# A reordered prologue for a chain of modulated convolutions, with products of zeros on TensorE in front of the first R and the first T

## The chip, the cores and the metric

The kernel runs on one core of one Trainium2 chip. The metric is the time of one launch in microseconds, as the median of several runs. The profile is one more execution, taken with the hardware profiler on. PE is TensorE's matmul row, PEld its weight loads, DVE is VectorE, ACT is ScalarE, POOL is GpSimd and SP the engine that issues most of the transfers.

## The reference, cut to what matters

Thirty-two samples of 64 channels and 1024 positions pass through four modulated 1-D convolutions with three taps (same, up by two with a blur, same, down by two with a blur). The result is added to the input. All of it is float32.

```python
def _layer(x, style, w, b, mw, mb, typ):
    s = style @ mw.T + mb
    weight = SCALE * w * s[:, None, :, None]
    demod = lax.rsqrt(jnp.sum(weight * weight, axis=(2, 3)) + EPS)
    weight = weight * demod[:, :, None, None]
    # 'same': conv, + b;  'upsample': transposed conv stride 2, + b, blur (1,3,3,1);
    # 'downsample': blur (1,3,3,1), conv stride 2, + b
out = x
for i, typ in enumerate(('same', 'upsample', 'same', 'downsample')):
    out = _layer(out, style, weights[i], biases[i], mod_w[i], mod_b[i], typ)
return x + out
```

## The kernel before, in words

The four layers are linear in the sample, so the kernel composes their taps into one filter per sample and applies that once. It works on eight groups of four samples (`QUADS`, index `q`). For a group, `compose_R` multiplies layer 2's taps (`V_st`) with layer 3's scaled taps (`A_sb`), `compose_H` brings in the blurred layer 1 (`F_st`) and `compose_T` layer 0 (`W0_st`). ACT empties PSUM after each, with the sample's scales (`evac_R`, `evac_H`, `evac_T`). The result is the filter `Tw`. DVE (first group) or POOL (later groups) adds the identity of the residual and sums of blocks to it (`add_ident`, `sum_blocks`). Then five products with the input follow, by a fast algorithm on differences of the input: `product_a2`, `product_bc2`, `product_a13`, `product_bc1`, `product_bc3`. Their moving operands are `x3` (ACT, `make_x3`), `dx_sb` (POOL, `make_dx`), `d_sb` and `dd_sb` (DVE, `make_d`, `make_dd`). DVE merges the products into the output tile (`make_s`, `make_e`, `finish`). In the loop over groups the work of group q+1 and q+2 on R, H and T stands between the products of group q.

Ahead of the loop stands a prologue, and the change is there. TensorE multiplies zeros four times (`pe_warm`, line 436), turns the modulation weights, forms the styles (452), turns the sums of squared weights (458), turns layer 3's taps (`put["GT"]`, 463), forms the demodulation sums (471) and blurs layer 1's taps in two parities (`blurred_taps`, 419, `put["FT"]`). Then come R of group 0, the turned taps of layers 0 and 2 (`transposed`, 410), R of group 1, a small product for the constant part (640), H of group 0, layer 3's blurred taps (`blurred_halves`, 429, for `o_st`), a second small product (649), the first of the edge products (`edge_x0`, 599), T of group 0, H of group 1, and the last small product (659, `put["oc"]`). The edges of the samples are computed apart in four small products, with POOL adding the offsets.

DVE makes the scales: styles, then `dt_`, then a square root on ACT (709), then `demodulation`, which refines it in four small instructions and yields `e2` (needed by `make_A`, hence by R), `a0` (by `evac_H`) and `id` (by `add_ident`). `s0` is a copy of the first layer's style that `evac_T` takes as its scale, `e1` the scale of `evac_R`. POOL copies `V_st` and `W0_st` out of the loaded weights, makes `dx_sb` for group 0, and builds `y_st`, the blurred taps for the edges, with `coef` and `prod`. The order of the work on each engine is written out by hand, and semaphores join the engines.

Of the kernel before, what the change touches and what calls it, by code (L numbers as in the profile page):

```python
# [10 lines left out]
P = 128  # L11
# [15 lines left out]
def modulated_conv_kernel(nc, x, cond, weights, biases, mod_w, mod_b, out):  # L27
# [18 lines left out]
    with ctx:  # L46
# [9 lines left out]
        def bufs(make, name, n, *a):  # L56
# [27 lines left out]
        coef = sb("coef", [C, len(BLUR), 1])  # L84
        prod = sb("prod", [C, K, len(BLUR), C])
# [61 lines left out]
                                            "GT", "FT", "oT", "x0e", "ye", "ze", "oe", "yc", "zc", "oc")}  # L147
        coef_made = sem("coef_made")
        blur_step = sem("blur_step")
        copied = {n: sem(f"copied_{n}") for n in ("styleT", "wsumT", "w0T", "G_mv", "V_st", "W0_st", "F_st", "w2T", "o_st")}  # L150
        made = {n: sem(f"made_{n}") for n in ("cid", "bias", "wsum", "style2", "s0", "dt", "e2", "e1", "a0", "vec", "y_st",
# [88 lines left out]
        def _(pool):  # L240
# [6 lines left out]
            for j, v in enumerate(BLUR):  # L247
                pool.memset(coef[:, j], v / 4).then_inc(coef_made, 1)
# [4 lines left out]
            pool.wait_ge(w_loaded, 16)  # L253
            for l, to, name in ((2, V_st, "V_st"), (0, W0_st, "W0_st")):
                of = wn[:, l].rearrange("o i k -> o k i")
                for h in range(2):
                    pool.tensor_copy(to[h * C:(h + 1) * C], of).then_inc(copied[name], 1)
                    pool.wait_ge(copied[name], h + 1)

            make_dx(pool, 0)  # L260

            pool.wait_ge(zeroed, 7)
            pool.wait_ge(coef_made, len(BLUR))
            n = len(BLUR)
            for k in range(K):
                pool.tensor_tensor(prod[:, k], wn[:, 1, :, k].unsqueeze(1).to_broadcast([C, n, C]),
                                   coef[:].to_broadcast([C, n, C]), ALU.mult).then_inc(blur_step, 1)
            for k in range(K):
                pool.wait_ge(blur_step, K + k)
                pool.tensor_tensor(y_st[0:C, k:k + n], y_st[0:C, k:k + n], prod[:, k], ALU.add).then_inc(blur_step, 1)  # L270
            pool.wait_ge(blur_step, 2 * K)
            pool.tensor_copy(y_st[C:P, 4:6], y_st[0:C, 2:4]).then_inc(made["y_st"], 1)

# [5 lines left out]
            pool.wait_ge(made["s0"], 1)  # L279
# [127 lines left out]
        def _(pe):  # L407
# [6 lines left out]
            def blurred_taps(l, bank, cid, n, par):  # L414

                for k in range(K):
                    for h in range(2):
                        b0 = 2 + par - k
                        ins = pe.matmul(bank[h * C:(h + 1) * C, 0:n * C], wn[:, l, :, k],
                                        cid[:, b0:b0 + 2 * n - 1:2, :], start=(k == 0), stop=(k == K - 1),  # L420
                                        skip_group_check=True)
                return ins
# [10 lines left out]

            pe.wait_ge(warm_made, 1)
            for _ in range(4):
                pe.matmul(p_h[:, 1, 0:256], pe_warm[:, 0:P], pe_warm[:], start=True, stop=True)
# [12 lines left out]
            ins.then_inc(put["bias"], 1)  # L449
            pe.wait_ge(copied["styleT"], 1)  # L450
# [4 lines left out]
            for half in (1, 0):  # L455
# [3 lines left out]
                ins.then_inc(put["wsumT"], 1)  # L459

# [5 lines left out]

            for half in (1, 0):
                pe.wait_ge(copied["wsumT"], 2 - half)
                pe.wait_ge(made["style2"], 1)
                for l in (2 * half, 2 * half + 1):  # L470
                    ins = pe.matmul(p_c[1 - half][0:C, 0, 256 + l * B:256 + (l + 1) * B], wsumT[:, l], style2[:, l, :],
                                    start=True, stop=True)
                ins.then_inc(put["demod"], 1)

            pe.wait_ge(made["cid"], 1)
            pe.wait_ge(made["s0"], 1)
            pe.wait_ge(made["bias"], 1)
# [126 lines left out]
            def edge_y():  # L604
                pe.wait_ge(made["x0e"], 1)
                pe.wait_ge(made["y_st"], 1)
# [29 lines left out]
            pe.wait_ge(copied["F_st"], 2)  # L636
            compose_R(1, p_h)
# [7 lines left out]
            blurred_halves(3, p_y[:, 1], cid1, 3).then_inc(put["oT"], 1)  # L645
            pe.wait_ge(made["z_st"], 6)
            pe.wait_ge(made["yc"], 1)
            for k in range(3):
                ins = pe.matmul(p_x[:, 1, 0:B], z_st[:, k, :], yc[:], start=(k == 0), stop=(k == 2))
            ins.then_inc(put["zc"], 1)  # L650
            pe.wait_ge(copied["w2T"], 1)
            edge_x0()
            compose_T(0)
            compose_H(1)
# [31 lines left out]
        def _(act):  # L686
# [8 lines left out]

            act.wait_ge(put["styleT"], 1)
# [8 lines left out]
            copy(G_mv[:], p_y[:, 1, 0:K * C].rearrange("p (a c) -> p a c", c=C), copied["G_mv"])  # L705
            for n, half in enumerate((1, 0)):
# [48 lines left out]
            act.wait_ge(put["FT"], 1)  # L755
            copy(F_st[:, 0:NF:2], p_x[:, 1, 0:5 * C].rearrange("p (a c) -> p a c", c=C), copied["F_st"], 1.0 / 32)
# [3 lines left out]
            act.wait_ge(put["FT"], 2)  # L760
            copy(F_st[:, 1:NF:2], p_h[:, 0, 0:4 * C].rearrange("p (a c) -> p a c", c=C), copied["F_st"], 1.0 / 32)
            make_A(1)
            act.wait_ge(made["e1"], 2)
            evac_R(0, p_k)
            act.wait_ge(put["w2T"], 1)
            copy(w0T[:], p_y[0:C, 0, 0:3 * C].rearrange("p (k c) -> p k c", c=C), copied["w0T"])
            copy(w2T[:], p_y[0:C, 0, 256:256 + 3 * C].rearrange("p (k c) -> p k c", c=C), copied["w2T"])
            evac_R(1, p_h)
            make_A(2)
# [22 lines left out]
        def _(dve):  # L792
# [48 lines left out]
            dve.wait_ge(put["bias"], 1)  # L841
            ts(biases2[:].rearrange("p j l -> p (j l)"), p_h[:, 1, 0:2 * LAYERS], 1.0, name="bias")
# [28 lines left out]
            for h, rows in enumerate(halves):  # L871
                ts(pgi(W_S0, h), gi(style[rows, 0], h), 1.0, name="s0")
            for n, half in enumerate((1, 0)):
                of = slice(2 * half, 2 * half + 2)
                dve.wait_ge(put["demod"], n + 1)
                for rows in halves:
                    ts(dt_[rows, of], p_c[1 - half][0:C, 0, 256 + 2 * half * B:256 + 2 * (half + 1) * B]
                       .rearrange("p (l b) -> p l b", b=B), SCALE2, EPS, ALU.mult, ALU.add, "dt")
            for h, rows in enumerate(halves):
                tt(pgi(W_E1, h), gi(style[rows, 2], h), gi(style[rows, 1], h), ALU.mult, "e1")  # L880

# [82 lines left out]
            for h, rows in enumerate(halves):  # L964
                tt(pgj(W_E2, h), gj(style[rows, 3], h), gj(dm[rows, 2], h), ALU.mult, "e2")
            dve.wait_ge(sqrt_done, 2)
# [3 lines left out]
            ts(vec[:, V_B0, 0:B], dm[:, 1, :], bias[:, 0:1], name="vec")  # L970
            demodulation(3, 4)
# [17 lines left out]
            make_d(0)  # L989
# [5 lines left out]
            dve.wait_ge(zeroed, 7)  # L995
            scale_edge("x0e", one_below_the_other(p_y), x0e[0:C], V_A0, WX0)
# [3 lines left out]
            sum_blocks(dve, 0)  # L1000
            dve.wait_ge(made["d3"], 2)
# [6 lines left out]
            make_dd(0)  # L1008

            for q in range(QUADS):  # L1010
                make_s(q)
                if q + 1 < QUADS:
                    make_d(q + 1)
# [6 lines left out]
                finish(q, 1, bank_bc3(q), bc3_done, y13_made)  # L1020
                if q + 1 < QUADS:
# [26 lines left out]
```

## Time and profile before

| | us |
|---|---|
| median of 3 runs | 163.07 (162.77 to 163.49) |
| the profiled execution, its own time | 164.6 |
| its span, first to last instruction | 162.5 |
| PE busy in the span | 149.3 |
| DVE busy | 117.5 |
| POOL busy | 68.7 |
| ACT busy | 57.1 |

The profiled execution took 1.1 us longer than the slowest of the three runs, and 2.1 us of its time lie outside the span. In the views, start and duration are microseconds from the span's start; a row of the timeline merges instructions of one kind in a row, with "x" for how many, and a matmul in float32 shows as two records. The granted clock is a share of TensorE's full 2.4 GHz, so 0.50 is 1.2 GHz.

### The profile page before, as it was taken

To read this page: it belongs to the slowest core of one execution; us is meant where nothing else is said; L and a number is where in the kernel's file an instruction comes from. 1 tells how busy PE (TensorE), PEld (TensorE's weight loads), DVE (VectorE), ACT (ScalarE), POOL (GpSimd) and SP (SyncE) were. 2 spreads that over 40 slices of the span, in tenths; PEclk is the share of its full clock that TensorE was granted. 3 is DMA by queue.
4 is the path that set the end of the run, shared out by engine and by line. 5 is a ranking of instruction groups with operands and counts; after the bars stand their busy time and mean duration, and the time that the engine had idled before them with its cause. 6 is when DMAs were issued, how large, how long until landed. Compare 5 with 4: busy or idle time off the path is not lost.

```text
span 162.5 us, 5859 instructions
## 1 busy us (share of the span) xinstructions
PE 149.3 (92%) x2585; PEld 117.5 (72%) x2585; DVE 117.5 (72%) x185; ACT 57.1 (35%) x118; POOL 68.7 (42%) x101
## 2 busy tenths in 40 slices
PE   7995999879999999999999999999999999989920
PEld 5562998555578656685889699879988997957810
DVE  7999745298786367697775877489747885789760
ACT  3222543545405512444346416541454234402000
POOL 8696060730385056692680086009402920540000
PEclk9965579999999999999999999999999999999995
DMA  4968100006001600059706920890190038005526
GB/s 122 346 152 225 53 0 4 0 4 237 25 0 21 249 0 4 0 183 325 268 11 135 292 97 0 200 316 11 31 226 9 4 68 193 6 0 114 148 48 210
DMA packets 9400, 17.62 MB, mean 108 GB/s; under 512 B 4736, under 2 KB 5280, under 8 KB 9376
## 3 DMA queue, kind: packets, MB, share of 16 engines
q1 hardware_dynamic: 9312, 17.24, 36.9%
q8 instruction: 20, 0.33, 0.8%
q14 instruction: 4, 0.03, 0.1%
q10 hardware_dynamic: 64, 0.02, 0.0%
HBM read 8.87 MB, written 8.39 MB: 106 GB/s over the span
## 4 chain that ended last, share of the span: by engine, by line
PE 78%; DVE 14%; issue 3%; ACT 1%; DVEq 0%; ACTq 0%
PE p_c L540 44%; PE p_k L507 11%; PE p_h L525 11%; PE p_k L490 5%; DVE e_sb L925 2%; DVE ot L937 2%; DVE pvec L815 1%; PE p_h L490 1%; DVE cid L815 1%; PE p_h L617 1%; PE p_h L610 1%; DVE pvec L811 1%; DVE Tw L214 1%; PE p_k L530 1%; DVE cid L828 1%
## 5 line engine op out<-in xcount | busy, mean ns | idle before, releaser
L540 PE MATMUL p_c<-dd_sb,Tw 64*64 64x256 f32 x504 | 30.3, 376 | 0.7 <-DVE e_sb L925 0.7
L925 DVE SCALAR_TENSOR_TENSOR e_sb<-p_c,pvec,s_sb 128x512 f32<-128x512 f32 x32 | 21.8, 744 | 7.3 <-PE p_c L540 7.3
L540 PEld LDWEIGHTS p_c<-dd_sb,Tw 64*64 64x64 f32 x504 | 22.4, 132 | 5.6 <-DVE e_sb L925 1.1
L214 POOL TENSOR_TENSOR Tw<-Tw,di_sb 128x128 f32<-128x128 f32 x7 | 3.2, 460 | 52.4 <-ACT Tw L738 52.4
L937 DVE SCALAR_TENSOR_TENSOR ot<-p_c,pvec,e_sb 128x508 f32<-128x508 f32 x28 | 19.9, 754 | 7.2 <-PE p_c L540 7.2
L507 PE MATMUL p_k<-R_sb,F_st 64*64 64x192 f32 (+1 forms) x576 | 22.1, 302 | 0.7 <-ACT Tw L735 0.7
L507 PEld LDWEIGHTS p_k<-R_sb,F_st 64*64 64x64 f32 x576 | 20.3, 135 | 1.4 <-issue 0.9
L914 DVE SCALAR_TENSOR_TENSOR s_sb<-p_c,pvec,t_sb 128x512 f32<-128x512 f32 x16 | 11.3, 746 | 12.9 <-PE p_c L540 12.9
L540 PE MATMUL p_c<-d_sb,Tw 64*64 64x256 f32 x320 | 19.9, 386 | 0.0
L906 DVE TENSOR_TENSOR dd_sb<-d_sb 128x2064 f32<-128x2064 f32 x8 | 19.9, 2487 | 0.0
L540 PE MATMUL p_c<-dx_sb,Tw 64*64 64x256 f32 x320 | 19.0, 376 | 0.3 <-DVE ot L937 0.3
L525 PE MATMUL p_h<-H_sb,W_st 64*64 64x448 f32 (+1 forms) x192 | 19.2, 518 | 0.0
L899 DVE TENSOR_TENSOR d_sb<-xin 128x2072 f32<-128x2072 f32 x8 | 18.4, 2306 | 0.0
L234 POOL TENSOR_TENSOR dx_sb<-xin 128x1032 f32<-128x1032 f32 x8 | 17.2, 2146 | 1.1 <-DMA xin<-in_x_dram 1.0
L540 PEld LDWEIGHTS p_c<-dx_sb,Tw 64*64 64x64 f32 x320 | 14.0, 133 | 3.7 <-issue 1.2
L540 PEld LDWEIGHTS p_c<-d_sb,Tw 64*64 64x64 f32 x320 | 13.7, 132 | 3.0
L721 ACT ACTIVATE R_sb<-p_k,pvec 128x320 f32<-128x320 f32 x14 | 6.6, 524 | 25.8 <-PE p_k L490 25.8
L752 ACT ACTIVATE t_sb<-p_c,pvec 128x256 f32<-128x256 f32 x16 | 8.2, 560 | 18.5 <-PE p_c L540 18.5
L525 PEld LDWEIGHTS p_h<-H_sb,W_st 64*64 64x64 f32 x192 | 8.8, 133 | 6.7 <-issue 6.2
L728 ACT ACTIVATE H_sb<-p_k,pvec 128x448 f32<-128x448 f32 x16 | 9.3, 630 | 11.3 <-PE p_k L507 11.3
L540 PE MATMUL p_c<-x,Tw 64*64 64x256 f32 x192 | 12.0, 376 | 1.0 <-DVE Tw L226 1.0
L735 ACT ACTIVATE Tw<-p_k,pvec 128x64 f32<-128x64 f32 x16 | 4.2, 310 | 21.5 <-PE p_k L530 21.5
(146 smaller groups left out, 195.3 us busy)
## 6 DMA issues: line engine op xcount, KB each, us to landing
xin<-in_x_dram SPq DMA_DIRECT2D x16, 512.0 KB, 5.3
out_dram<-ot SPq DMA_DIRECT2D x14, 512.0 KB, 6.2
out_dram<-ot SPq DMA_DIRECT2D x4, 256.0 KB, 3.5
wn<-in_L_cond_weights_dram SPq DMA_DIRECT2D x1, 192.0 KB, 3.5
mwn<-in_L_cond_mod_w_dram SPq DMA_DIRECT2D x1, 128.0 KB, 2.3
xe<-in_x_dram SPq DMA_DIRECT2D x2, 64.0 KB, 9.4
cn<-in_cond_dram ACTq DMA_DIRECT2D x1, 16.0 KB, 2.2
bn<-in_L_cond_mod_b_dram ACTq DMA_DIRECT2D x1, 1.0 KB
```

The costliest lines, as they stand in the source:

```text
L234: eng.tensor_tensor(dx_sb[q % 2][:], view(a, 1, ((XW, 2), (4, 2), (4, NI))), view(a, 3, ((XW, 2), (0, 2), (4, NI))), ALU.subtract).then_in ...
L490: ins = pe.matmul(bank[i * C:(i + 1) * C, j, b * C:(b + K) * C], V_st[rows, K - 1 - b, :], A_sb[q % 2][rows, i], start=(b == 0), stop=(b = ...
L507: ins = pe.matmul(p_k[j * C:(j + 1) * C, i, to * C:(to + n) * C], F_st[rows, f, :], R_sb[q % 2][rows, j, par::2], start=(f == 0), stop=(f ...
L525: pe.matmul(p_h[i * C:(i + 1) * C, j, first * C:(first + n) * C], W0_st[rows, k, :], H_sb[rows, i, 0:n], start=(k == 2), stop=(k == 0), sk ...
L540: ins = pe.matmul(bank[j * C:(j + 1) * C, i], Tw[q % NW][rows, blk, j, :], moving(rows, j, n), start=(n == 0), stop=(n == len(blocks) - 1) ...
L728: act.activation(H_sb[:, i], p_k[:, i, 0:NH * C].rearrange("p (a c) -> p a c", c=C), ACT.Copy, scale=pcol(W_A0, 2 * q + i)).then_inc(H_eva ...
L752: act.activation(t_sb[q % 2][:, i], p_c[q % 2][:, i, 0:NQ], ACT.Identity, bias=pcol(W_C, 2 * q + i), scale=pcol(W_D3, 2 * q + i)).then_inc ...
L899: dve.tensor_tensor(d_sb[q % 2][:], view(a, 0, ((XW, 2), (2, 2), (2, ND))), view(a, 1, ((XW, 2), (0, 2), (2, ND))), ALU.subtract).then_inc ...
L906: dve.tensor_tensor(dd_sb[:].rearrange("p j t s n -> p (j t) s n"), view(a, 0, ((ND, 4), (2, 2), (2, NI))), view(a, 1, ((ND, 4), (0, 2), ( ...
L914: dve.scalar_tensor_tensor(out=s_sb[:, i], in0=p_c[(q + 1) % 2][:, i].rearrange("p (n h) -> p n h", h=2), scalar=pcol(W_D3, 2 * q + i), in ...
L925: dve.scalar_tensor_tensor(out=e_sb[:, i, w], in0=p_c[q % 2][:, i, w * NQ:(w + 1) * NQ].unsqueeze(2) .to_broadcast([P, NQ, 2]), scalar=pco ...
L937: dve.scalar_tensor_tensor(out=ot[q % NO_T][:, i, 4 + par:4 + par + 2 * n - 1:2], in0=bank[:, i, 2:2 + n], scalar=pcol(W_D3, 2 * q + i), i ...
```

## The change

The prologue is put in another order. POOL no longer copies `V_st` and `W0_st` (ACT does) nor builds `y_st` (four products on TensorE and two copies on ACT do), and its `make_dx(0)` waits for `a0`. On TensorE the blurred taps of the first parity are spread over three places, the demodulation sums come ahead of layer 3's turned taps, the turned taps of layers 0 and 2 come ahead of R, and `edge_x0` and the second small product come behind T of group 0. On ACT `evac_T(0)` follows `make_x3(0)`, and the two square roots follow the copies of `G_mv` and of half of `F_st`. On DVE `s0`, `e1`, `make_d(0)`, `make_dd(0)`, `make_d(1)` and the edge scaling of `x0e` come later. `keep_busy` multiplies zeros: three times ahead of R of group 0, once ahead of T of group 0.

```diff
 # POOL
-            pool.wait_ge(w_loaded, 16)
-            for l, to, name in ((2, V_st, "V_st"), (0, W0_st, "W0_st")):
-                    pool.tensor_copy(to[h * C:(h + 1) * C], of).then_inc(copied[name], 1)
+            pool.wait_ge(made["a0"], 2)
             make_dx(pool, 0)
-            for k in range(K):
-                pool.tensor_tensor(prod[:, k], wn[:, 1, :, k]..., coef[:]..., ALU.mult).then_inc(blur_step, 1)
-            for k in range(K):
-                pool.tensor_tensor(y_st[0:C, k:k + n], y_st[0:C, k:k + n], prod[:, k], ALU.add).then_inc(blur_step, 1)
-            pool.tensor_copy(y_st[C:P, 4:6], y_st[0:C, 2:4]).then_inc(made["y_st"], 1)
 # TensorE
+            def keep_busy(bank, times, n):
+                for _ in range(times):
+                    pe.matmul(bank[:, 0:n], pe_warm[:, 0:P], pe_warm[:, 0:n], start=True, stop=True)
+            blurred_taps(1, p_h[:, 0], cid2, 5, 0, 0)            # ahead of the styles
+            sums_turned(1)
+            sums_turned(0)
+            blurred_taps(1, p_h[:, 0], cid2, 5, 0, 1)
+            (demodulation sums, then GT)
-            pe.wait_ge(made["s0"], 1)
-            blurred_taps(1, p_x[:, 1], cid2, 5, 0).then_inc(put["FT"], 1)
-            blurred_taps(1, p_h[:, 0], cid2, 4, 1).then_inc(put["FT"], 1)
+            blurred_taps(1, p_h[:, 0], cid2, 5, 0, 2).then_inc(put["FT"], 1)
+            for k in range(K):
+                ins = blurred_taps(1, p_x[:, 0], cid2, 4, 1, k)
+            ins.then_inc(put["FT"], 1)
+            transposed(0, p_y[:, 0], 0)
+            transposed(2, p_y[:, 0], 256).then_inc(put["w2T"], 1)
+            pe.wait_ge(made["dt"], 4)
+            for j in range(len(BLUR)):
+                ins = pe.matmul(p_x[0:C, 1, j * C:(j + K) * C], cid1[:, 2 + j], wn[:, 1].rearrange("o i k -> o k i"),
+                                start=(j == 0), stop=(j == len(BLUR) - 1), skip_group_check=True)
+            ins.then_inc(put["yst"], 1)
...
+            pe.wait_ge(made["bias"], 1)
+            keep_busy(p_h[:, 1], 3, 256)
             compose_R(0, p_k)
-            transposed(0, p_y[:, 0], 0)
-            transposed(2, p_y[:, 0], 256).then_inc(put["w2T"], 1)
             pe.wait_ge(copied["F_st"], 2)
             compose_R(1, p_h)
...
             blurred_halves(3, p_y[:, 1], cid1, 3).then_inc(put["oT"], 1)
+            pe.wait_ge(R_evac, 4)
+            keep_busy(p_h[:, 1], 1, 256)
+            compose_T(0)
             (second small product, line 649 before)
+            compose_H(1)
             edge_x0()
-            compose_T(0)
-            compose_H(1)
 # ACT
+            act.wait_ge(w_loaded, 16)
+            copy_taps(2, V_st, "V_st")                           # ahead of the modulation weights
...
             copy(G_mv[:], ...)
+            act.wait_ge(put["FT"], 1)
+            copy(F_st[:, 0:NF:2], p_h[:, 0, 0:5 * C]..., copied["F_st"], 1.0 / 32)
             (the two square roots)
...
+            (F_st of the other parity, w2T, then make_A(0), make_A(1), the two copies into y_st)
             evac_R(0, p_k)
             evac_R(1, p_h)
-            make_A(2)
+            copy_taps(0, W0_st, "W0_st")
             evac_H(0)
+            make_x3(0)
+            act.wait_ge(made["s0"], 2)
             evac_T(0)
-            make_x3(0)
+            make_A(2)
             evac_H(1)
 # DVE
-            (s0 ahead of dt, e1 ahead of the demodulation; now behind a0 and behind e2)
-            make_d(0)
             (zc)
-            scale_edge("x0e", ...)
             add_ident(dve, 0)
             sum_blocks(dve, 0)
+            scale_edge("x0e", ...)
             (the two steps of W_C, named "c")
-            make_dd(0)
+            make_d(0)
             for q in range(QUADS):
                 make_s(q)
+                if q == 0:
+                    make_dd(0)
...
                 finish(q, 1, bank_bc3(q), bc3_done, y13_made)
+                if q == 0:
+                    make_d(1)
```

## Rows read from the trace of the kernel before

**Rows 1.** The chain of waits in order of time: start, duration, what ran.
```profile
15.43 0.81 ACT A_sb L715 x2
...
16.37 2.20 PE p_k L490 x24
...
35.26 3.69 PE p_c L540 x64
...
47.49 0.97 PE p_k L490 x24
...
51.49 2.50 PE p_k L507 x72
```

**Rows 2.** Timeline of TensorE's matmuls, 0 to 37 us.
```profile
1.20 3.78 PE L436 MATMUL p_h<-pe_warm 128*128 128x256 f32 x8 [1.20 <-DVE pe_warm L822]
...
7.47 0.75 PE L463 MATMUL p_c<-ident,wn 64*64 64x64 f32 x12
...
8.66 3.28 PE L419 MATMUL p_c<-cid,wn 64*64 64x320 f32 x12
11.66 2.84 PE L419 MATMUL p_h<-cid,wn 64*64 64x256 f32 x12
...
18.32 1.37 PE L410 MATMUL p_c<-ident,wn 64*64 64x64 f32 x11
...
24.79 1.23 PE L429 MATMUL p_c<-cid,wn 64*64 64x192 f32 x12
...
26.73 1.16 PE L599 MATMUL p_c<-xse,w0T 64*64 64x224 f32 x9
...
27.91 2.31 PE L525 MATMUL p_h<-H_sb,W_st 64*64 64x448 f32 x21
...
31.09 2.73 PE L507 MATMUL p_k<-R_sb,F_st 64*64 64x192 f32 x72 [0.74 <-ACT Tw L735]
33.75 0.54 PE L659 MATMUL p_c<-zc,o_st 128*64 128x32 f32 x12
...
36.60 2.34 PE L540 MATMUL p_c<-dx_sb,Tw 64*64 64x256 f32 x40
...
41.03 2.46 PE L540 MATMUL p_c<-d_sb,Tw 64*64 64x256 f32 x40
```

**Rows 3.** Stretches: engines' busy us, granted clock, DMA share, GB/s.
```profile
9.00:9.50 0.50, 0.50 (x4) 0.30 (x2) 0.50 (x1) 0.00 (x0) 0.50 (x1) 0.50 1.14 248
...
22.00:22.50 0.50, 0.50 (x11) 0.50 (x14) 0.16 (x1) 0.50 (x2) 0.50 (x2) 0.50 0.00 0
...
23.00:23.50 0.50, 0.50 (x21) 0.50 (x17) 0.50 (x5) 0.43 (x2) 0.16 (x1) 1.00 0.00 0
```

**Rows 4.** Timeline of DVE in the prologue.
```profile
8.39 2.12 DVE L815 TENSOR_SCALAR pvec<-style 64x16 f32<-64x16 f32 x2
...
23.57 2.30 DVE L899 TENSOR_TENSOR d_sb<-xin 128x2072 f32<-128x2072 f32 x1
...
28.20 0.81 DVE L811 TENSOR_TENSOR x0e<-p_c,vec 64x224 f32<-64x224 f32 x2 [0.88 <-PE p_c L599]
28.93 0.28 DVE L208 TENSOR_TENSOR di_sb<-ident,pvec 128x128 f32<-128x128 f32 x1
32.13 1.21 DVE L214 TENSOR_TENSOR Tw<-Tw,di_sb 128x128 f32<-128x128 f32 x1 [2.92 <-ACT Tw L738]
```

**Rows 5.** Timeline of POOL in the prologue.
```profile
8.40 2.08 POOL L234 TENSOR_TENSOR dx_sb<-xin 128x1032 f32<-128x1032 f32 x1 [0.98 <-DMA xin<-in_x_dram]
...
29.09 1.23 POOL L298 TENSOR_TENSOR x0e<-x0e,vec 64x224 f32<-64x224 f32 x2 [5.92 <-DVE x0e L811]
...
31.01 2.17 POOL L234 TENSOR_TENSOR dx_sb<-xin 128x1032 f32<-128x1032 f32 x1
```

**Rows 6.** Timeline of ACT in the prologue.
```profile
25.19 1.16 ACT L728 ACTIVATE H_sb<-p_k,pvec 128x448 f32<-128x448 f32 x2 [1.75 <-PE p_k L507]
...
30.42 0.52 ACT L735 ACTIVATE Tw<-p_k,pvec 128x64 f32<-128x64 f32 x2 [3.86 <-PE p_k L530]
```

More of the change, by code:

```diff
@@ L146, in modulated_conv_kernel @@
         put = {n: sem(f"put_{n}") for n in ("styleT", "bias", "w2T", "wsumT", "style", "demod",
[L147 to L151, printed above, removed]
+                                            "GT", "FT", "oT", "yst", "x0e", "ye", "ze", "oe", "yc", "zc", "oc")}
+        copied = {n: sem(f"copied_{n}") for n in ("styleT", "wsumT", "w0T", "G_mv", "V_st", "W0_st", "F_st", "w2T", "o_st", "y_st")}
+        made = {n: sem(f"made_{n}") for n in ("cid", "bias", "wsum", "style2", "s0", "dt", "e2", "e1", "a0", "vec",
                                               "z_st", "zc", "xse", "x0e", "ye", "ze", "yc", "c", "oe", "oep", "e_read",
@@ L277, in _ @@
                 pool.tensor_copy(dst, w2T[:, k]).then_inc(made["z_st"], 1)
-            pool.wait_ge(made["s0"], 1)
+            pool.wait_ge(made["z_st"], 6)
+            pool.wait_ge(made["style2"], 1)
             pool.wait_ge(e_loaded, 32)
@@ L412, in transposed, with blurred_taps @@
                 return ins
[L414 to L421, printed above, removed]
+            def blurred_taps(l, bank, cid, n, par, k):
+                for h in range(2):
+                    b0 = 2 + par - k
+                    ins = pe.matmul(bank[h * C:(h + 1) * C, 0:n * C], wn[:, l, :, k],
+                                    cid[:, b0:b0 + 2 * n - 1:2, :], start=(k == 0), stop=(k == K - 1),
+                                    skip_group_check=True)
                 return ins
@@ L432, in blurred_halves @@
                 return ins
+            def keep_busy(bank, times, n):
+                for _ in range(times):
+                    pe.matmul(bank[:, 0:n], pe_warm[:, 0:P], pe_warm[:, 0:n], start=True, stop=True)
             pe.wait_ge(warm_made, 1)
-            for _ in range(4):
-                pe.matmul(p_h[:, 1, 0:256], pe_warm[:, 0:P], pe_warm[:], start=True, stop=True)
+            keep_busy(p_h[:, 1], 4, 256)
             pe.wait_ge(ident_made, 1)
@@ L449, in _ @@
             ins.then_inc(put["bias"], 1)
+            pe.wait_ge(w_loaded, 16)
+            pe.wait_ge(made["cid"], 1)
+            blurred_taps(1, p_h[:, 0], cid2, 5, 0, 0)
             pe.wait_ge(copied["styleT"], 1)
@@ L453, in _, with sums_turned @@
             ins.then_inc(put["style"], 1)
-            for half in (1, 0):
+            def sums_turned(half):
                 pe.wait_ge(made["wsum"], 2 - half)
@@ L459, in _ @@
                 ins.then_inc(put["wsumT"], 1)
+            sums_turned(1)
+            sums_turned(0)
+            blurred_taps(1, p_h[:, 0], cid2, 5, 0, 1)
+            for half in (1, 0):
+                pe.wait_ge(copied["wsumT"], 2 - half)
+                pe.wait_ge(made["style2"], 1)
+                for l in (2 * half, 2 * half + 1):
+                    ins = pe.matmul(p_k[0:C, half, 256 + l * B:256 + (l + 1) * B], wsumT[:, l], style2[:, l, :],
+                                    start=True, stop=True)
+                ins.then_inc(put["demod"], 1)
             for a in range(K):
@@ L605, in edge_y @@
                 pe.wait_ge(made["x0e"], 1)
-                pe.wait_ge(made["y_st"], 1)
+                pe.wait_ge(copied["y_st"], 2)
                 pe.wait_ge(T_evac, 8)
@@ L694, in _, with copy_taps @@
             act.activation(sqrt_warm[:], xin[0][:, 0, 0:1], ACT.Sqrt)
+            def copy_taps(l, to, name):
+                for h in range(2):
+                    copy(to[h * C:(h + 1) * C], wn[:, l].rearrange("o i k -> o k i"), copied[name])
+            act.wait_ge(w_loaded, 16)
+            copy_taps(2, V_st, "V_st")
             act.wait_ge(put["styleT"], 1)
@@ L870, in _ @@
             dve.wait_ge(dve_step, n_style)
-            for h, rows in enumerate(halves):
-                ts(pgi(W_S0, h), gi(style[rows, 0], h), 1.0, name="s0")
             for n, half in enumerate((1, 0)):
@@ L876, in _ @@
                 for rows in halves:
-                    ts(dt_[rows, of], p_c[1 - half][0:C, 0, 256 + 2 * half * B:256 + 2 * (half + 1) * B]
+                    ts(dt_[rows, of], p_k[0:C, half, 256 + 2 * half * B:256 + 2 * (half + 1) * B]
                        .rearrange("p (l b) -> p l b", b=B), SCALE2, EPS, ALU.mult, ALU.add, "dt")
-            for h, rows in enumerate(halves):
-                tt(pgi(W_E1, h), gi(style[rows, 2], h), gi(style[rows, 1], h), ALU.mult, "e1")
             def demodulation(l0, l1):
@@ L965, in _ @@
                 tt(pgj(W_E2, h), gj(style[rows, 3], h), gj(dm[rows, 2], h), ALU.mult, "e2")
+            for h, rows in enumerate(halves):
+                tt(pgi(W_E1, h), gi(style[rows, 2], h), gi(style[rows, 1], h), ALU.mult, "e1")
             dve.wait_ge(sqrt_done, 2)
@@ L970, in _ @@
             ts(vec[:, V_B0, 0:B], dm[:, 1, :], bias[:, 0:1], name="vec")
+            for h, rows in enumerate(halves):
+                ts(pgi(W_S0, h), gi(style[rows, 0], h), 1.0, name="s0")
             demodulation(3, 4)
@@ L1000, in _ @@
             sum_blocks(dve, 0)
+            dve.wait_ge(zeroed, 7)
+            scale_edge("x0e", one_below_the_other(p_y), x0e[0:C], V_A0, WX0)
             dve.wait_ge(made["d3"], 2)
```

51 lines of the change are left out of this document (16 added, 35 removed).

## The prediction

> **What bounds the kernel now.** I read the chain of waits first. From 35 us to about 140 us it is TensorE with hardly a break, its products, R, H and T one behind the other in an order written by hand; two of its rows are R of a later group at 0.97 us and H at 2.50 us [rows 1]. Nothing in that stretch is changed except the place of DVE's differences for the first two groups. So the change is worth what it moves the start of the first group's second product, 36.60 in the timeline [rows 2], if no new wait follows. Ahead of it the chain goes through ACT's A (ends at 16.23), R at 16.37, and the first product at 35.26 [rows 1].
>
> Then the stretches with their clock: 0.50, the 1.2 GHz level, from 9.0 us to about 22.5, and 1.00 from 23.0 [rows 3]. Line 419 ran through the fall and stayed at the low level, twelve records in the 3.00 us from 8.66 to 11.66. The level rose after both first R and the start of H. In the first five microseconds the column says 1.00, but the eight records of zeros took 3.78 us, 0.47 us each for 256 columns, which is the low level's pace [rows 2].
>
> Last, DVE beside POOL. Two copies of 64x16 (`s0`) took 2.12 us, ending with POOL's `dx_sb` at 10.48; the first step on `Tw` took 1.21 us, where another of 128x128 took 0.28, ending just behind POOL's next `dx_sb` at 33.18 [rows 4, 5]. So instructions of the two on SBUF exclude each other here.
>
> **The change part by part, up to R.** On DVE the stall of 1.9 us behind `dx_sb` leaves (`s0` moves behind `a0`), and `y_st` no longer competes with the demodulation. A, made at 16.23 before, could be there at 14.3 or earlier. But TensorE now has more to do ahead of R. Its first eight records of blurred taps fit where it waits for the styles and their squares, so I leave the end of the demodulation sums at 8.66. From there, in order:
>
> - Layer 3's turned taps, 0.75 us [rows 2]: to 9.4.
> - Four records of the third tap, 0.25 each: 1.0.
> - Twelve of the other parity: 3.00 x 256/320 = 2.4, or 2.84 by their own row with its drain; 2.5.
> - Twelve turned taps of layers 0 and 2: eleven took 1.37; 1.3.
> - `y_st`, eight records of 192 columns on one tile alone, not in the trace. By the zeros 0.47 x 192/256 = 0.35 each, by the turned taps three times 0.11 or 0.12; 2.6 with the drain left out. Bounds: 1.3 at the high level, 2.8.
> - Zeros, six records: 3.78 x 6/8 = 2.8 with the drain, 2.6 without; 1.3 at the high level.
>
> At the low level that is 10.0 us, so R starts at 19.4, not 16.37. ACT makes A behind the copy of w2T, whose product ends at 9.4 + 4.8 = 14.2, so A is done near 15.6. By this TensorE does not wait in front of R at all; it would get there at 16.8 without the zeros, and they stand on the path for 2.6 us. The copies that ACT takes over from POOL lie in its waits ahead of the styles and ahead of H; uncovered they'd cost a few tenths each.
>
> What the zeros buy is the clock. Before, R took 1.95 us at the low level (16.37 to 18.32), later 0.97 [rows 1, 2]. If the level rises as R starts, both R and the small product behind them (0.35, an estimate: six records of two thirds of the last small product's twelve) end at 19.4 + 0.97 + 0.97 + 0.35 = 21.7, ACT emptying the first R beside the second, and H, 2.50, at 24.2. Before, H ended at 24.79, where line 429 starts. That is 0.6 gained. If both R still run low, H ends 1.96 later, at 26.15: 1.4 lost. The first zeros, four products, ran low to their end; the level after them was high by line 419's start at the latest. I take the rise inside the first R, at a third: 0.3 later, H's end at 24.5.
>
> The Trainium skill, page "TensorE: Matmul & The Clock Gate", Part 1, says that the default state is throttled and activity releases the throttle. The trace agrees for the first zeros but not for line 419, busy without a gap for 5.8 us and low throughout [rows 2, 3]. By that rule alone the new prologue, in which TensorE hardly pauses, would run high and end near 156.8; by the row it runs low to R, 162.0.
>
> **From H's end, called h.** ACT's copies of H end at 25.19 + 1.16, which is h + 1.56 [rows 6]. TensorE fills this with line 429 (1.0 without its drain) and the one product of zeros (two records of 0.47 at the low pace of line 436, half at the high one, 0.5): hidden, and 0.4 late if the level is low; and `edge_x0` no longer stands in front of T. T starts at h + 1.6. From T's start to ACT's first copy it is 2.5 (27.91 to 30.42), from there to DVE's first step 1.7: h + 5.8. DVE's sums took 3.13 us to 35.26; with POOL idle the first takes 0.28 instead of 1.21, so they end at h + 8.0. TensorE meanwhile runs H of group 1 (0.67 behind the first copy, 2.66 long) to h + 7.45, `edge_x0` 1.18 to h + 8.6, the last small product 0.45 to h + 9.05 [rows 2]. The first product starts there, against h + 10.47 before, and ends 1.34 later, h + 10.4.
>
> The second product then waits for `c`, and that chain is late now: DVE's x0e starts 1.47 behind `edge_x0`'s start, at h + 8.9, and ends at h + 9.7 [rows 2, 4]. Two steps from PSUM of 64x16 take 0.4, two more on SBUF as much (estimate: the pair of `s0` without its stall, 0.2 each), but POOL starts its two sums of x0e, 0.6 each [rows 5], so each comes behind one of these: `c` at h + 11.05. Without that contention it would be h + 10.5, and the wait 0.1. I take 11.1, against 36.60 - 24.79 = 11.8 before. Gain 0.7.
>
> The rest is covered: `make_d(0)`, 2.30, ends near h + 14, and the third product needs it 4.43 behind the second's start (36.60 to 41.03), at h + 15.5. `make_dd(0)` has the third product and the edge product in front of its reader. In group 0's end DVE makes two differences in a row while TensorE runs the next group's first product, H and second. POOL now waits for `a0`, which comes with A, near 15; queued behind that wait are `dx_sb` (2.08), the copies into `z_st` and the edge scaling `xse`, whose readers stand behind T, 10 us later. SP and its transfers are not moved, and its next loads that look at these differences belong to groups 4 and later.
>
> Sum: 0.6 - 0.3 + 0.7 = 1.0 us. The profiled execution's 164.6 would be 163.6; the median lies 1.5 under the profiled one, so from 163.07 I come to **162.0**. Half a per cent, about 0.8 us, is what a measurement can tell here.
>
> **The rivals.**
>
> - *The clock rises too late.* R and R of group 1 run low as they did before [rows 3], and the zeros only delay them: 1.4 lost, 0.7 won, 163.8. It decides from where both R have more than about 0.7 us of low level behind the forecast. For it: the rise came only behind both R before. Against it: then 1.2 us of turned taps on single tiles stood between them, now the zeros lead straight in. Chance 0.25, spread from 162.4 to 163.9.
> - *The clock does not fall at 9.* The products of blurred taps in the waits keep the level, all 10.0 us take 5.0, R starts at 14.4, and A (14.3 or earlier) is just there. Gain 0.6 + 0.7 + 5.0 = 6.3: 156.8. For it: TensorE is much busier between 5.5 and 9 than before. Against it: line 419 alone didn't raise the level. Chance 0.2; a fall one stretch later would land between.
> - *POOL's second difference goes in front of `make_d(0)`.* Both ask for SBUF near h + 11.6. If POOL's 2.17 goes first, d ends at h + 16.1, the third product is 0.6 late: 162.6. Chance 0.1.
> - *The zeros do nothing*, because R waits for A longer than I think: A past 19.4 would be 3.8 late. R is then where it is anyway and the other gains stay; its chance is inside the forecast's.
>
> The forecast itself has 0.45, from 161.5 (no contention for `c`, rise at R's start) to 162.4. Faster by over 0.5%: most of the forecast 0.38, the clock that stays 0.2, a little of the others: 0.6. Within: 0.06 + 0.13 + 0.08, 0.27. Slower: half of the late rise, 0.13. The range, 157.0 to 163.6, leaves out the lower half of the clock that stays (0.1) and the last of the late rise (0.08).
>
> **What would show it.** The clock should read 0.50 from about 9 to 19 and 1.00 by 20.5; the first R near 19.4, lasting under 1.5 us; line 436's new records 0.43 us apart; no wait of R for A. T should start 1.6 behind H, DVE's first step on `Tw` take 0.3, and the second product wait for `c` about 0.7. R near 14.4 with a high clock, or a low clock past 21, would make the forecast wrong.

## The result, and the profile after

The changed kernel takes 165.06 us (median of 4, 164.70 to 166.93), the kernel before 163.26 beside it (162.77 to 163.49): 1.0094, with a 95% interval of 1.0049 to 1.0140. It is slower by 0.9%, where 162.0 was forecast. Twelve more executions of the same kernel gave 165.12 against 163.37, 1.0056 (1.0024 to 1.0089). Executions over 1.5% above the fastest of their kernel count in the medians here, but not in the ratios.

The profiled execution of after took 166.93 us, the longest of its six, with a span of 164.9. So I show the profile of the repeated run too (165.56, span 163.8), which is nearer the median.

Timeline of TensorE's matmuls in the profile after (start, duration, line, what, how many records; in brackets a wait), beside [rows 2]:

```profile
6.07 1.33 PE L396 MATMUL p_h<-cid,wn 64*64 64x320 f32 x4
7.33 1.06 PE L436 MATMUL p_c<-cT,mwT 128*64 128x32 f32 x8
...
8.88 1.33 PE L396 MATMUL p_h<-cid,wn 64*64 64x320 f32 x4
10.01 0.89 PE L453 MATMUL p_k<-style,wsumT 64*64 64x32 f32 x7
...
12.41 2.92 PE L396 MATMUL p_c<-cid,wn 64*64 64x256 f32 x12
15.12 1.48 PE L388 MATMUL p_c<-ident,wn 64*64 64x64 f32 x12
16.41 2.76 PE L470 MATMUL p_c<-wn,cid 64*64 64x192 f32 x8
19.10 2.93 PE L414 MATMUL p_h<-pe_warm 128*128 128x256 f32 x6
21.95 1.94 PE L483 MATMUL p_k<-A_sb,V_st 64*64 64x192 f32 x24
23.72 1.15 PE L483 MATMUL p_h<-A_sb,V_st 64*64 64x192 f32 x24
...
27.58 1.24 PE L406 MATMUL p_c<-cid,wn 64*64 64x192 f32 x12
28.75 0.70 PE L414 MATMUL p_h<-pe_warm 128*128 128x256 f32 x2
29.39 2.38 PE L518 MATMUL p_h<-H_sb,W_st 64*64 64x448 f32 x24
...
36.92 1.53 PE L533 MATMUL p_c<-x,Tw 64*64 64x256 f32 x24
38.88 2.40 PE L533 MATMUL p_c<-dx_sb,Tw 64*64 64x256 f32 x40 [0.43 <-issue]
```

No row from 6.07 to 36.92 has a bracket: no wait of TensorE shows there. The zeros (L414, 19.10) and then R (L483, 21.95) begin as soon as the row ahead ends. R began at 16.37 before, so it is 5.6 later; the second product, 36.60 before, is 2.3 later, nearly as much as the span grew (164.9 against 162.5). From the second product to the end of the span it is 125.9 us before and 126.0 after: the loss is made ahead of it.

The chain of waits in the same profile, where [rows 1] had ACT's A just ahead of R:

```profile
6.14 1.26 PE p_h L396 x4
...
8.96 1.26 PE p_h L396 x4
...
12.77 2.56 PE p_c L396 x12
15.33 1.28 PE p_c L388 x12
16.61 2.56 PE p_c L470 x8
19.17 2.86 PE p_h L414 x6
22.02 1.86 PE p_k L483 x24
```

From 6.14 to R it is TensorE alone. ACT and POOL are out of it, as their own timelines show, beside [rows 5, 6]: A for the first two groups, on ACT, is done at 18.35, 3.6 ahead of R, and POOL's difference starts as soon as `a0` is there.

```profile
16.87 1.48 ACT L720 ACTIVATE A_sb<-G_mv,pvec 128x192 f32<-128x192 f32 x4
```
```profile
17.17 2.06 POOL L230 TENSOR_TENSOR dx_sb<-xin 128x1032 f32<-128x1032 f32 x1 [12.94 <-DVE pvec L820]
```

DVE, beside [rows 4]: it waits for the styles on TensorE (1.04 ahead of 8.43), `s0` stalls behind POOL once more (2.25, harmless here), and the first step on `Tw` takes 0.29 instead of 1.21.

```profile
8.43 0.28 DVE L820 TENSOR_TENSOR style<-p_c,biases 64x128 f32<-64x128 f32 x1 [1.04 <-PE p_c L436]
...
17.22 2.25 DVE L824 TENSOR_SCALAR pvec<-style 64x16 f32<-64x16 f32 x2
...
33.71 0.29 DVE L210 TENSOR_TENSOR Tw<-Tw,di_sb 128x128 f32<-128x128 f32 x1 [0.32 <-ACT Tw L743]
```

For the clock I read the repeated run, by stretches as in [rows 3] (the last three columns are granted clock, DMA share and GB/s). In after's own profile the column says 1.00 up to the rise, though the zeros took 0.48 us a record there, the low level's pace; its first entry stands at 23.49.

```profile
9.00:9.50 0.50, 0.50 (x4) 0.23 (x1) 0.00 (x0) 0.00 (x0) 0.00 (x0) 0.50 0.99 317
21.00:21.50 0.50, 0.50 (x2) 0.00 (x0) 0.47 (x2) 0.00 (x0) 0.50 (x2) 0.50 0.00 0
21.50:22.00 0.50, 0.50 (x11) 0.43 (x14) 0.47 (x3) 0.00 (x0) 0.29 (x1) 0.76 0.00 0
```

And the repeated run's TensorE:

```profile
5.85 0.79 PE L396 MATMUL p_h<-cid,wn 64*64 64x320 f32 x4
7.32 0.65 PE L436 MATMUL p_c<-cT,mwT 128*64 128x32 f32 x8 [0.68 <-ACT mwT L684]
...
8.46 1.33 PE L396 MATMUL p_h<-cid,wn 64*64 64x320 f32 x4
9.58 0.90 PE L453 MATMUL p_k<-style,wsumT 64*64 64x32 f32 x7
...
18.68 2.93 PE L414 MATMUL p_h<-pe_warm 128*128 128x256 f32 x6
21.54 1.28 PE L483 MATMUL p_k<-A_sb,V_st 64*64 64x192 f32 x24
...
37.80 2.39 PE L533 MATMUL p_c<-dx_sb,Tw 64*64 64x256 f32 x40 [0.42 <-issue]
```

Here the clock was high from 4.67 to 8.09 and from 21.74 (the trace's own entries for the clock, finer than the stretches). Four records of blurred taps (L396) take 0.79 in the high stretch and 1.33 behind it. So one kernel gives two prologues, by where the level changes.

The wait of 0.68 ahead of the styles (L436) has a cause that before had not. ACT now copies `V_st` before it copies the turned modulation weights (`mwT`, 6.89 to 7.27), and that copy waits for the weights to land:

```profile
5.81 0.97 ACT L684 ACTIVATE V_st<-wn 64x192 f32<-64x192 f32 x2 [2.16 <-DMA wn<-in_L_cond_weights_dram]
```

In the nine other profiles in which ACT makes this copy it starts between 4.59 and 4.91, so the late landing belongs to this execution. In before's profile `mwT` was copied at 5.88 without a look at these weights, and the styles stood at 6.32:

```profile
6.32 0.65 PE L452 MATMUL p_c<-cT,mwT 128*64 128x32 f32 x8 [0.35 <-ACT mwT L688]
```

The mean granted clock, known for every execution, sorts the executions; these are 12 and 29 on one chip:

| mean clock | changed, us | before, us (median) |
|---|---|---|
| .960 to .963 | 163.68 to 164.02 (4) | 162.80 to 164.16 (12; 163.1) |
| .944 to .952 | 164.98 to 165.56 (6) | 164.01 to 164.59 (6; 164.1) |
| .985 to .987 | 167.26 and 167.42 (2) | 163.05 to 164.01 (8; 163.4) |

The three executions of before that are left out lay at .953 (two) and .991. At a like clock the change loses 0.6, 1.0 and 3.9 us. After's profile is of the third kind, whose high mean comes from the column's 1.00 ahead of its first entry. The executions of the changed kernel at .961, and the five at .944 and .945 that set its median, have no profile.

### The profile page after: what moved, and what is told of

It reads as the page before. It is cut to its first block, busy times and chain, and to the rows that moved or that the text cites. A ratio compares the mean times of both kernels' runs of the same rounds, so it can differ in the third digit from the quotient of the medians.

```text
span 164.9 us, 5884 instructions
## 1 busy us (share of the span) xinstructions
PE 155.2 (94%) x2601; PEld 119.0 (72%) x2601; DVE 116.8 (71%) x185; ACT 59.4 (36%) x124; POOL 65.5 (40%) x86
## 4 chain that ended last, share of the span: by engine, by line
PE 90%; DVE 4%; issue 2%; DVEq 0%
PE p_c L533 43%; PE p_k L500 12%; PE p_h L518 11%; PE p_k L483 5%; PE p_h L414 4%; DVE e_sb L930 2%; PE p_h L396 2%; DVE ot L942 2%; PE p_c L396 2%; PE p_c L470 2%; PE p_h L610 1%; PE p_h L603 1%; PE p_c L388 1%; PE p_c L592 1%; PE p_c L436 1%
## 5 line engine op out<-in xcount | busy, mean ns | idle before, releaser
L533 PEld LDWEIGHTS p_c<-dd_sb,Tw 64*64 64x64 f32 x504 | 21.8, 132 | 6.2 <-DVE e_sb L930 1.1
L911 DVE TENSOR_TENSOR dd_sb<-d_sb 128x2064 f32<-128x2064 f32 x8 | 21.0, 2626 | 0.0
L500 PEld LDWEIGHTS p_k<-R_sb,F_st 64*64 64x64 f32 x576 | 19.8, 133 | 0.8
L518 PEld LDWEIGHTS p_h<-H_sb,W_st 64*64 64x64 f32 x192 | 8.3, 133 | 7.3 <-issue 6.4
```

Of the source, the lines that this page charges most:

```text
L500: ins = pe.matmul(p_k[j * C:(j + 1) * C, i, to * C:(to + n) * C], F_st[rows, f, :], R_sb[q % 2][rows, j, par::2], start=(f == 0), stop=(f ...
L518: pe.matmul(p_h[i * C:(i + 1) * C, j, first * C:(first + n) * C], W0_st[rows, k, :], H_sb[rows, i, 0:n], start=(k == 2), stop=(k == 0), sk ...
L533: ins = pe.matmul(bank[j * C:(j + 1) * C, i], Tw[q % NW][rows, blk, j, :], moving(rows, j, n), start=(n == 0), stop=(n == len(blocks) - 1) ...
L911: dve.tensor_tensor(dd_sb[:].rearrange("p j t s n -> p (j t) s n"), view(a, 0, ((ND, 4), (2, 2), (2, NI))), view(a, 1, ((ND, 4), (0, 2), ( ...
```

## The experiments

**Theory.** From 6 us to the first R TensorE's own queue is the path, so zeros there cost about their duration, and the earlier rise doesn't pay for it. **Rival.** The zeros cost nothing (something else would hold R, or they bring the rise forward by as much), and the new order of the prologue is what is slower. Kernels without zeros leave out no part of the result: nobody reads what those products write. Each ratio is to the kernel before on the same chip. The runs come from three chips, on which the median of before lay between 163.03 and 163.37.

**Without the zeros ahead of R.**

```diff
-            keep_busy(p_h[:, 1], 3, 256)
             compose_R(0, p_k)
```

> The changed kernel without the three products of zeros ahead of the first R. Theory 1 (TensorE's queue is the path ahead of R, the zeros stand on it): the first R starts 2.5 us earlier than with them, the level rises at about the same time or up to 2 us later, and the kernel takes 0.5 to 2.5 us less than the changed one, 163.0 +- 0.8, beside the kernel before. Theory 2 (the zeros are hidden, or they pay for themselves with the clock): both R and H run low behind them, and the time is that of the changed kernel, 165, or more.

162.09 us; ratio to before 0.9950 (0.9917 to 0.9984), against 1.0094 and 1.0056 with the zeros. So three products of zeros cost 1.1 to 1.4%, about 2 us, more than the whole loss. Its profile is of the same kind as after's (taps 1.33, high level only from 21.0), and so they can be laid side by side: R at 18.34 instead of 21.95 (three records of it stand ahead of the last one of `y_st`, the others behind it from 18.71), the second product at 36.10 instead of 38.88, 2.78 earlier, and 164.2 us instead of 166.9. From R's start to the second product it is 17.76 us without the zeros and 16.93 with them, so they give back 0.8. They did not bring the rise forward in time: it came at 21.00 without them and at 23.49 with them, only nearer to R. The theory holds.

```profile
8.89 1.33 PE L396 MATMUL p_h<-cid,wn 64*64 64x320 f32 x4
...
18.34 0.59 PE L483 MATMUL p_k<-A_sb,V_st 64*64 64x192 f32 x3
...
36.10 2.39 PE L533 MATMUL p_c<-dx_sb,Tw 64*64 64x256 f32 x40 [0.43 <-issue]
```

**Without the zeros ahead of T.**

```diff
-            keep_busy(p_h[:, 1], 1, 256)
             compose_T(0)
```

> The changed kernel without the one product of zeros ahead of the first T. Theory 1: it lies in the wait for ACT's copies of H, so nothing changes (within 0.4 us of the changed kernel). Theory 2 (it delays T, as its records end when T starts): 0.4 us less.

1.0054 (1.0012 to 1.0095): as the changed kernel. The median is 165.83, because six of the twelve executions were of the third kind of the table, 166.64 to 167.22; why so many is not shown. Kind by kind the executions lie 0.1 to 0.6 us under those of the changed kernel. In the profiles, both of the third kind, T starts at 29.23 instead of 29.39, so most of these zeros (0.70) stand in a wait that is there anyway.

**Without any zeros.** Both edits together.

> The changed kernel with no zeros but the old four: the reordered order alone. Theory 1: as without the first zeros, 163.0 +- 0.8; what is left over the kernel before then belongs to the order (products of taps and of y_st ahead of R). Theory 2: 165 or more.

162.69; 0.9972 (0.9931 to 1.0012), no different from leaving out the first alone. By these two ratios the new order without the zeros is worth 0.3 to 0.5%, or, as the second interval reaches 1.0012, perhaps nothing; it is no loss that could explain the 0.9%: the rival's second half falls. Its profile had the early high stretch (5.55 to 8.96) in the place where before's had it, and shows what my forecast had assumed:

```profile
5.90 0.79 PE L396 MATMUL p_h<-cid,wn 64*64 64x320 f32 x4
6.62 0.65 PE L436 MATMUL p_c<-cT,mwT 128*64 128x32 f32 x8
...
7.54 0.79 PE L396 MATMUL p_h<-cid,wn 64*64 64x320 f32 x4
8.16 0.54 PE L453 MATMUL p_k<-style,wsumT 64*64 64x32 f32 x7
...
14.11 2.44 PE L470 MATMUL p_c<-wn,cid 64*64 64x192 f32 x7
16.04 0.59 PE L483 MATMUL p_k<-A_sb,V_st 64*64 64x192 f32 x3
```

The demodulation sums start at 8.16, not 10.01, and R comes at 16.04, ahead of the last record of `y_st`. In after's profile the zeros start 2.69 behind the first product for `y_st` (L470), and R 5.54 behind it. By that R with the zeros would come here at 14.11 + 5.54 = 19.65 (an estimate), near the 19.4 of the forecast.

**The kernel before, with three products of zeros ahead of R.**

```diff
+            for _ in range(3):
+                pe.matmul(p_h[:, 1, 0:256], pe_warm[:, 0:P], pe_warm[:], start=True, stop=True)
             compose_R(0, p_k)
```

> The kernel before with the three products of zeros ahead of its first R, where it waits 1.9 us for A. Theory 1: 2.6 us of zeros at the low level overrun the wait by 0.7 us, the rise of the clock comes up to 2 us earlier relative to R: between 1.0 less and 1.3 us more than the kernel before. Theory 2 (zeros in a wait are free and warm the clock): 1 to 2 us less than the kernel before.

1.0128 (1.0077 to 1.0179), 2.1 us more. This is where zeros should have been cheapest, since TensorE waited 1.87 ahead of R. But in the profiled execution the blurred taps ran later (10.28 instead of 8.66) and ended at 16.3, behind A (15.9). So there was no wait to fill, and the zeros go on top. The other executions of this kernel have no profile; whether the wait was there in some of them is not shown.

```profile
16.23 2.93 PE L634 MATMUL p_h<-pe_warm 128*128 128x256 f32 x6
19.09 1.57 PE L490 MATMUL p_k<-A_sb,V_st 64*64 64x192 f32 x24
```

The level rose at 19.88, inside R, just as intended, and H ended at 25.33, still later than 24.79 in [rows 2]. By the ratio, which counts the other executions too, the rival falls.

**Six products instead of three.**

```diff
-            keep_busy(p_h[:, 1], 3, 256)
+            keep_busy(p_h[:, 1], 6, 256)
```

> The changed kernel with six products of zeros ahead of the first R instead of three. Theory 1 (the zeros lie on the path, and what they give back through the clock is less): three more take 2.6 us at the low level or 1.3 at the high one, and the earlier rise gives at most 2.0 back on the two R: 0.3 to 2.6 us more than the changed kernel. Theory 2 (more zeros raise the level before R and pay): less time than the changed kernel.

168.44 (165.3 to 168.6, four executions, no interval). The level rose at 24.23, so both R run at the high level, from 24.41 on (first R 1.21 long); 168.5 stands against the 166.9 of after's profile, and 165.3 against 163.8: 1.5 for 2.4 us more of zeros. The median rose by 3.4, more than expected, as three of the four were of the long kind.

**No zeros, and the early taps gathered back.** The question: is it the taps in the waits that make the rest late?

```diff
-            blurred_taps(1, p_h[:, 0], cid2, 5, 0, 0)     # ahead of the styles
-            blurred_taps(1, p_h[:, 0], cid2, 5, 0, 1)     # ahead of the demodulation sums
...
+            blurred_taps(1, p_h[:, 0], cid2, 5, 0, 0)
+            blurred_taps(1, p_h[:, 0], cid2, 5, 0, 1)
             blurred_taps(1, p_h[:, 0], cid2, 5, 0, 2).then_inc(put["FT"], 1)
```

> Without zeros, and the two early groups of blurred taps put back beside the third, behind layer 3's turned taps. Theory 1: TensorE's queue is the path, so it matters only how much of the styles' waits they filled: 0 to 1.2 us more than the order without zeros (162.7). Rival (they delay styles and demodulation, and these are the path): 0.5 to 2 us less.

1.0112 (1.0069 to 1.0156), against 0.9972 for the same without this edit; at a clock near .947 164.5 against 163.5. That is more than the 0 to 1.2 us expected. The waits come back (0.34 and 0.22) and R starts at 18.80. Its profile has no early high stretch, nor has that of the first experiment, where R stood at 18.34. So R itself is only 0.46 later, while the level rises 2.68 later (23.68 against 21.00) and the second product comes 1.30 later (37.40 against 36.10). Taps in the waits, then, are not the loss. How much of what they are worth comes from the queue, and how much from an earlier rise, is not separated.

**No zeros, and the products for `y_st` behind H, ahead of T.**

```diff
-            (four products for y_st, ahead of R)
...
             blurred_halves(3, p_y[:, 1], cid1, 3).then_inc(put["oT"], 1)
+            (four products for y_st)
             pe.wait_ge(R_evac, 4)
```

> Without zeros, and the four products for y_st and ACT's two copies of them moved from ahead of R to behind layer 3's blurred taps, where the first T waits for ACT. Theory 1: 2.6 us of low level leave the path ahead of R and 0.7 come back ahead of T; the rise of the clock doesn't come earlier by as much: 0.3 to 1.9 us less than the order without zeros (162.7). Rival (the first R waits for A then): nothing gained.

1.0040 (1.0002 to 1.0078), no gain over 0.9972. This is a miss of the theory as I put it, and the rival's outcome: with `y_st` gone, R waits 1.20 for ACT's A, and the products are on the path ahead of T, at 24.50.

```profile
15.89 2.20 PE L479 MATMUL p_k<-A_sb,V_st 64*64 64x192 f32 x24 [1.20 <-ACT A_sb L719]
```

**All that R doesn't need behind both R, and A ahead of the copies.** The taps of the other parity and the turned taps go behind R of group 1, `y_st` ahead of T, layer 3's turned taps ahead of the demodulation sums; ACT takes the square roots and A ahead of both copies of `F_st`. No zeros.

```diff
 # TensorE
...
             compose_R(0, p_k)
-            pe.wait_ge(copied["F_st"], 2)
+            pe.wait_ge(copied["F_st"], 1)
             compose_R(1, p_h)
+            for k in range(K):
+                ins = blurred_taps(1, p_x[:, 0], cid2, 4, 1, k)
+            ins.then_inc(put["FT"], 1)
+            transposed(0, p_y[:, 0], 0)
+            transposed(2, p_y[:, 0], 256).then_inc(put["w2T"], 1)
+            pe.wait_ge(copied["F_st"], 2)
+            compose_H(0)
...
```

> As the one before, and more of TensorE's work put behind the first two R: the taps of the other parity and the turned taps of layers 0 and 2. The early taps are beside the third, layer 3's turned taps ahead of the demodulation sums, and ACT takes the square roots and A ahead of its copies of F_st. Theory 1: the first R starts near 12.5 us, and H 3 to 5 us earlier than in the order without zeros: 159 to 161.5. Rival (H gets no earlier, since the same work stands ahead of it at the low level): 162 to 163.

161.68; **0.9916 (0.9879 to 0.9953)**, ahead of both kernels, and just above the 159 to 161.5 expected. R starts at 12.83, without a wait:

```profile
12.83 2.20 PE L474 MATMUL p_k<-A_sb,V_st 64*64 64x192 f32 x24
14.78 2.18 PE L474 MATMUL p_h<-A_sb,V_st 64*64 64x192 f32 x24
16.70 1.57 PE L396 MATMUL p_c<-cid,wn 64*64 64x256 f32 x12
...
34.58 2.39 PE L524 MATMUL p_c<-dx_sb,Tw 64*64 64x256 f32 x40 [0.42 <-issue]
```

Both R run low, and that costs less than what warming up for them did. The high level begins at 16.87, so the moved taps take 1.57 instead of 2.92. Beside the first experiment's profile, which has no early high stretch either, H ends 3.2 earlier (21.6 against 24.8), but the second product comes only 1.5 earlier (34.58 against 36.10), since `y_st` now stands between H and T. The edits were made together, and no run tells what each is worth.

**The kernel before, with DVE's and POOL's part of the change alone** (`s0` and `e1` later, POOL's difference behind `a0`).

```diff
 # POOL
+            pool.wait_ge(made["a0"], 2)
             make_dx(pool, 0)
 # DVE: the steps for s0 and e1 go behind a0 and e2
```

> The kernel before with the DVE and POOL part of the change alone: POOL's first difference and its y_st behind a0, s0 behind vec, e1 behind e2; TensorE's and ACT's order untouched. Theory 1: A is ready by the end of the blurred taps, so R starts at 14.5 instead of 16.4 and the kernel takes 1.0 to 1.9 us less than before. Rival (the level is low longer behind an earlier R, or y_st behind a0 is late for its reader): within 0.5 us of before.

1.0034 (1.0005 to 1.0063), where the theory had a gain: a miss. R did start earlier, at 14.12 instead of 16.37. But TensorE waits ahead of `edge_x0`. The bracket names no cause, but the wait ends as POOL's edge scaling `xse` does, at 25.2:

```profile
25.32 1.13 PE L600 MATMUL p_c<-xse,w0T 64*64 64x224 f32 x9 [1.32 <-issue]
```
```profile
21.80 3.42 POOL L283 TENSOR_TENSOR xse<-xe,style 64x288 f32<-64x288 f32 x2
```
```profile
21.88 2.80 DVE L897 TENSOR_TENSOR d_sb<-xin 128x2072 f32<-128x2072 f32 x1
```

Before, `xse` started at the same time and took 1.32:

```profile
21.85 1.32 POOL L282 TENSOR_TENSOR xse<-xe,style 64x288 f32<-64x288 f32 x2
```

So it is not a later start that makes `xse` late, but its length beside DVE's `make_d(0)`, which comes earlier now (23.57 before). That wait doesn't explain the missing gain either: in this profile the second product still comes 1.45 earlier (35.15 against 36.60), and the execution takes 163.18, where before's profile took 164.6. It is the shortest of the twelve. Of the others those at .948 and .949 take 163.3 to 164.0, where before takes 164.0 to 164.6; those at .961 take 163.7 to 164.1, where before's median is 163.1. Why they don't keep the gain that this profile shows is open.

In the changed kernel `make_d(0)` stands much later and `edge_x0` behind T, so this wait isn't in it.

**The best order, with six products of zeros at the very start instead of four.**

```diff
-            keep_busy(p_h[:, 1], 4, 256)
+            keep_busy(p_h[:, 1], 6, 256)
```

> The faster order (work behind R, no zeros ahead of R and T) with six products of zeros at the very start instead of four, where TensorE waits for the first loads. Theory 1: two more end at 6.3 if all run low, the styles come 0.5 to 1 us later, and in return the high level is there in more executions: 161.7 +- 0.7, with less spread. Rival (they only delay): 1 us more.

0.9975 (0.9954 to 0.9997), against 0.9916. They move the styles from 6.48 to 7.67 and R to 13.28. By the two ratios that is 1.0 us more, as the rival had it. Eleven of twelve executions lie within 1.1 us, though: a steadier time, and a longer one.

**The changed kernel once more**, for a second profile; its result stands in the first section (0.6% more, at 163.7, 165.1 and 167.3).

> The changed kernel itself once more, for more executions beside the kernel before on the same chip: 0.9% more, with the time set by where the level rises: 163.8, 165.0 or 166.9.

## Why the prediction was wrong

The forecast was 162.0, the result 165.06. Point by point:

- *TensorE does not wait in front of R, and the zeros stand on the path*: right, by the chain, and by the first experiment. In after's profile their duration was 2.86 (forecast 2.6), `y_st` 2.56 (2.6), the other parity 2.56 (2.5), the turned taps 1.28 (1.3). A came at 18.35, not 15.6, still 3.6 ahead of its need.
- ***"Its first eight records of blurred taps fit where it waits for the styles and their squares, so I leave the end of the demodulation sums at 8.66"***: this step failed. It holds where the early high stretch covers them, as in the profile without zeros (sums start at 8.16). In after's profile there was no such stretch: the taps took 1.26 twice, the styles came at 7.33 instead of 6.32, and the sums ended near 11.0. In the repeated one they ended at 10.6, for two reasons. The first taps ran high, but then TensorE waited 0.68 for ACT, which stood behind the late weights with its copy of `V_st`; so *"the copies that ACT takes over from POOL lie in its waits"* failed there as well. And the stretch ended at 8.09, so that the second taps ran low. In the profile with `y_st` ahead of T, whose order up to these sums is the same, the weights were there in time and the level was high to 8.02: there the sums ended at 9.1. From their end to R I was within 0.2 us, so R came at 21.54 and 21.95, not at 19.4.
- *"I take the rise inside the first R, at a third"*: in the repeated run it came inside the first R (21.74, R 1.28 long). In after's profile it came as that R ended; R took 1.94, and H ended 5.63 behind R's start instead of 5.1. The rival "the clock rises too late" describes that one execution, and the time it gave, 163.8, is 3.1 short of it, because its R starts late as well.
- *From H's end*: right. T at h + 1.8 (1.6), the first step on `Tw` 0.29 (0.28), second product at h + 11.30 (11.1), with a wait of 0.43 for `c` (about 0.7), whose two steps on SBUF took 0.90 beside POOL and ended at 38.78, just ahead of that product's 38.88. Neither of POOL's differences got in front of `make_d(0)`: that rival didn't happen.
- *"The profiled one would be 163.6; the median lies 1.5 under"*: the second half failed. The profile before was not a typical execution with something added; it was one of .948, a kind that takes 164.0 to 164.6, while the twelve at .96 took 163.1 in the median (none of these has a profile). Of the changed kernel ten of eighteen executions lay between .943 and .952, where before has 6 of 29. The 163.6 is near what its shortest executions take (163.7 to 164.0), but they are of another kind, so this is no support for the sum.

The sum closes: in after's profile H ends at 27.58 instead of 24.5 (3.1) and the second product comes 0.2 later from there; 163.6 + 3.3 = 166.9, the time that it took. In the repeated one 2.0 at H's end and 0.2 make 165.8, against 165.56. The median can be split by the table. Among executions between .944 and .952 the kernel takes 165.1 against 164.1, where the sum had 1.0 less: 2.0 of the 3.1 us by which it was missed. The other 1.1 come from the offset: the 163.07 that the forecast started from is the time of before's executions at .96 (163.1), and the median of the changed kernel lies in the slower kind. In the repeated profile the 2.0 stand at H's end and come from R's late start, about 0.7 of them from the wait for ACT. How they divide in the executions at .944, which have no profile, is not shown.

The rival of the clock that doesn't fall at 9 fell: every profile with an early high stretch lost it again before 10 us, and in all of them the blurred taps that followed ran at the low level, though TensorE hardly paused (from 6 us to the fall no single wait of it was over 0.68). The Trainium skill's rule (page "TensorE: Matmul & The Clock Gate", Part 1) that activity releases the throttle is not borne out for them. That the point of the rise differs between executions of one kernel is in the same section of the Trainium skill, and the two profiles of the changed kernel agree: 23.49 and 21.74.

What the zeros were to buy was bounded in my own sum: both R at the low level cost 1.96 us, and the zeros last 2.6 to 2.9. By that sum they could only lose against a kernel that has the new order without them; I set them against the kernel before, and hid that loss in the gain of the order. Not settled is why so many executions of the changed kernel are of the slower kinds; no run varied that alone.

## What to carry to other kernels

Price an insertion against the same kernel without it, not against the one before: its best gain (here 1.96 us of low clock) must exceed its duration on the queue (2.86). Where the engine's queue is the path, move what the next stage doesn't need behind it, and let it run at the clock that comes by itself; only waits that are there anyway may be filled. An engine that takes over a copy takes over what the copy waits for, and so does all that stands behind it: here the styles came to depend on the landing of the weights. When a profile's time isn't the median, find out first which kind of execution it shows, since an offset taken over to the changed kernel can be off by as much as the change is worth.

## What the runs showed that I had not expected

The column of the granted clock reads 1.00 ahead of its first entry whatever the level is, so an execution with a mean of .986 can be the one that ran lowest; the pace of known products (0.47 to 0.49 us for a record of zeros of 256 columns) tells. The same kernel took 163.7, 165.1 or 167.3 us, by where the level changed, while all but three of before's 29 lay within 1.8 us. Perhaps the work on the path ahead of R makes a kernel more sensitive to it; no run shows that by itself. And instructions of DVE and POOL on SBUF still exclude each other in new places: `s0` took 2.25 beside `dx_sb`, POOL's copy of `x0e` 2.74 beside `make_d(0)` (0.55 before), and in the kernel before with DVE's and POOL's part `xse` 3.42 instead of 1.32.
